# A transformer block's state-space stage: x, z and gates from rounded high and low parts, two buffers for the convolution, weights split in the stage before, and one set of expert weights loaded later

## The reference, cut to what matters

```
normed = layernorm(x, ln1_g, ln1_b)
r = normed @ Wr + br
alpha = sigmoid(r[..., 0:1])
xs, z = split(normed @ Win, 2)
y = causal depthwise convolution of xs with 4 taps, + cb
ssm_out = (silu(y) * sigmoid(z)) @ Wout
gate = sigmoid(normed @ Wgate)          # of the attention branch
blended = ls1 * ((1 - alpha) * ssm_out + alpha * attn_out)
```

## Time and profile before

| what | us |
|---|---|
| median of 3 runs (1224.36 to 1227.06) | 1226.8 |
| the profiled execution | 1225.03 |
| its span, first to last instruction | 1223.3 |
| merge phase | 505 to 536 |
| state-space phase | 536 to 598 |
| self-attention phase | 599 to 729 |
| busy over the span: TensorE, VectorE, ScalarE, GpSimd | 1081.9, 783.1, 649.1, 801.1 |

### The profile page before, as it was taken

The page is one execution under the profiler, slowest core; times in us unless marked ns, Lnnn a source line. Parts: engine busy times, 40 slices in busy tenths (PEclk is TensorE's granted clock), DMA queues, the critical chain, the costliest instruction groups (busy, mean ns, idle before and its releaser), DMA issues. The chain is left out here.

```text
span 1223.3 us, 27556 instructions
## 1 busy us (share of the span) xinstructions
PE 1081.9 (88%) x8144; PEld 973.9 (80%) x8145; DVE 783.1 (64%) x2337; ACT 649.1 (53%) x1499; POOL 801.1 (65%) x835
## 2 busy tenths in 40 slices
PE   4799999999999999879889954899999833999998
PEld 2599999999999999768667743688888622899897
DVE  5566666666666666565456558976776556664663
ACT  1565655655556565153367755766666442553451
POOL 0487777777777778224578750677777503789895
PEclk9899999999999999789899986899999965999999
DMA  4212111111221211089000032133333247645520
GB/s 115 78 53 70 56 56 52 53 54 52 62 63 52 68 57 46 28 214 371 7 1 0 0 59 83 34 53 52 52 52 52 39 143 226 191 119 113 156 45 10
DMA packets 72147, 94.27 MB, mean 77 GB/s; under 512 B 14828, under 2 KB 52160, under 8 KB 72096
## 3 DMA queue, kind: packets, MB, share of 16 engines
q1 hardware_dynamic: 53584, 73.00, 18.7%
q0 software_dynamic: 16032, 20.62, 10.5%
q10 hardware_dynamic: 2480, 0.03, 0.1%
HBM read 73.69 MB, written 22.18 MB: 78 GB/s over the span
## 5 line engine op out<-in xcount | busy, mean ns | idle before, releaser
L1860 POOL DMA_INDIRECT e_x<-rows,source x71 | 76.1, 1071 | 102.1 <-DMA rows<-weight 40.3
L428 PE MATMUL xa_ob<-xa_v,xa_pT 128*128 128x65 f32 x1024 | 135.1, 276 | 0.2 <-DVE xa_pT L653 0.2
L495 POOL TENSOR_TENSOR xa_qbd<-qs,xw_c_mask8s 128x512 fp32r<-128x512 f32 x128 | 131.8, 1051 | 2.3 <-ACT xa_pr L583 2.2
L566 ACT ACTIVATE xa_kT<-xa_kvp,xw_bk 128x258 fp32r<-128x258 f32 x128 | 61.2, 478 | 131.5 <-PE xa_kvp L382 123.9
L583 ACT ACTIVATE xa_pr<-xa_pr,xa_nm 128x257 f32<-128x257 f32 x256 | 109.6, 500 | 34.4 <-DVE xa_nm L649 34.3
L428 PEld LDWEIGHTS xa_ob<-xa_v,xa_pT 128*128 128x128 f32 x1024 | 126.5, 194 | 0.3 <-DVE xa_pT L653 0.3
L642 DVE TENSOR_SCALAR_CACHE_REDUCE xa_pr<-xa_sc 128x257 f32<-128x257 f32 x256 | 98.1, 421 | 23.4 <-PE xa_sc L408 23.4
L525 POOL TENSOR_TENSOR xa_ol<-xa_om,xa_tl 128x256 f32<-128x256 f32 x64 | 47.1, 736 | 81.7 <-DVE xa_rinv L670 81.5
L1865 POOL DMA_INDIRECT base<-e_y,place x39 | 71.6, 1837 | 36.4 <-DVE e_y L2148 19.5
L2527 PE MATMUL e_hb<-e_xTs,e_w1s 128*128 128x512 f32 x384 | 90.9, 396 | 1.9 <-issue 1.9
L653 DVE TENSOR_SCALAR xa_pT<-xa_ptp 128x512 f32<-128x512 f32 x128 | 87.7, 685 | 7.2 <-PE xa_ptp L417 3.2
(11 more groups left out here) (360 smaller groups left out, 3289.9 us busy)
## 6 DMA issues: line engine op xcount, KB each, us to landing
e_w<-in_F_W SPq DMA_DIRECT2D x16, 1024.0 KB, 8.0
w<-in_W SPq DMA_DIRECT2D x24, 512.0 KB, 8.7
xa_ctx<-in_ctxT SPq DMA_DIRECT2D x32, 257.0 KB, 3.0
xa_ctx<-in_ctxT SPq DMA_DIRECT2D x64, 128.5 KB, 3.1
xa_vb<-vlx SPq DMA_DIRECT2D x64, 128.0 KB
rows<-xs_oT SPq DMA_DIRECT2D x8, 512.0 KB, 4.4
xs_oT<-in_x SPq DMA_DIRECT2D x4, 512.0 KB, 5.8
base<-xs_oT SPq DMA_DIRECT2D x4, 512.0 KB, 3.4
```

Source lines behind the costliest of these rows:

```text
L428: mm = pe.matmul(ob[:, 65 * g:65 * g + 65], pT[:, par, g, t, :], v[:, vs, t, g, :], start=(g == 0 and t == 0), stop=(g == G - 1 and t == 1 ...
L495: pool.tensor_tensor(dst, src, msk, ALU.mult).then_inc(q_ready, 1)
L1860: return pool.indirect_dma_start(out=out, out_offset=None, in_=rows, in_offset=bass.IndirectOffsetOnAxis(ap=index, axis=0))
```

## The change

In the state-space phase x, z and the gates are made from parts. A number is split into a high part, rounded to the type fp32r by writing it in that type, and a low part, the rest. A product is then three matmuls in fp32r: high by high, high by low, low by high. The weights are split by GpSimd at the beginning of the merge phase (`split_state_space_weights`: two copies and two subtractions), and SyncE issues the loads of the weights ahead of all else in that phase. The rows of step 0 are split by GpSimd in the merge phase too (`split_first_rows`), behind `nT_stored` 2 and ahead of its four DMAs. The rows of every later step are split in the step before: ScalarE writes the high part, at the head of its step, and GpSimd subtracts. The copy to `nS` goes away.

`xp`, `y` and `sz` get two buffers. So the copy of x waits for the convolution two steps back, and the convolution for yz and sy of two steps back. GpSimd waits with yz for the convolution and Sigmoid of z, and for sy only ahead of gT. The last two steps are written out, and the loop has two turns.

The parts, y and sz lie in the place of `w2`, the first experts' W2, which is therefore loaded by SyncE at the start of the self-attention phase.

```diff
@@ merge_phase
         @block.sync
         def _(sp):
+            load_early(sp)
             for i in range(NG):
                 sp.wait_ge(x1_ready, 2 * i + 2)
                 sp.dma_start(base[...], xs[...]).then_inc(base_written[i], 16)
-                if i == 0:
-                    load_early(sp)
         @block.gpsimd
         def _(pool):
+            split_early(pool)
+            pool.wait_ge(nT_stored, 2)
+            split_rows(pool)
             for i in range(NG):
...
+def split_state_space_weights(pool, w, parts):
+    pool.wait_ge(w.loaded, w.total)
+    for a, b in ((w["Wzx"], parts["zx"]), (w["Wgr"], parts["gr"])):
+        pool.tensor_copy(b[:, 0], a[:]).then_inc(parts["high"], 1)
+    for n, (a, b) in enumerate(((w["Wzx"], parts["zx"]), (w["Wgr"], parts["gr"]))):
+        pool.wait_ge(parts["high"], n + 1)
+        pool.tensor_tensor(b[:, 1], a[:], b[:, 0], ALU.subtract).then_inc(parts["low"], 1)
+
+def split_first_rows(pool, nT, parts):
+    pool.tensor_copy(parts["nS"][:, 0, 0], nT[:, :, 0:V2]).then_inc(parts["nh_ready"], 1)
+    pool.wait_ge(parts["nh_ready"], 1)
+    pool.tensor_tensor(parts["nS"][:, 0, 1], nT[:, :, 0:V2], parts["nS"][:, 0, 0], ALU.subtract).then_inc(parts["nl_ready"], 1)
...
@@ state_space_phase
-        xp = p.sb("ss_xp", [P, 2, BS, L + 3])
+        xp = p.sb("ss_xp", [P, 2, 2, BS, L + 3])
+        TERMS = [(k, a, b) for k in range(2) for a, b in ((0, 0), (0, 1), (1, 0))]
...
         @block.tensor
-                        for k in range(2):
-                            mm = pe.matmul(bank[:, h, :], wzx[:, k, o + P * h:o + P * h + P], src[k],
-                                           start=(k == 0), stop=(k == 1))
+                        for n, (k, a, b) in enumerate(TERMS):
+                            mm = pe.matmul(bank[:, h, :], wzx[:, a, k, o + P * h:o + P * h + P], nS[:, par, b, k, :],
+                                           start=(n == 0), stop=(n == 5))
...
-                    for k in range(2):
-                        lhs = nS[:, par, k, P * t:P * t + P]
-                        mm = pe.matmul(gb[:, t, 0:D + 2], lhs, wgr[:, k, :], start=(k == 0), stop=(k == 1))
+                    for n, (k, a, b) in enumerate(TERMS):
+                        mm = pe.matmul(gb[:, t, 0:D + 2], nS[:, par, a, k, P * t:P * t + P], wgr[:, b, k, :],
+                                       start=(n == 0), stop=(n == 5))
...
         @block.gpsimd
+            def low_part(s, par):
+                pool.wait_ge(parts["nh_ready"], s + 1)
+                pool.tensor_tensor(nS[:, par, 1], nT[:, :, bass.ds(s * V2, V2)], nS[:, par, 0], ALU.subtract
+                                   ).then_inc(parts["nl_ready"], 1)
             def step(s, par):
-                pool.tensor_copy(nS[:, par], nT[:, :, bass.ds(s * V2, V2)]).then_inc(nS_ready, 1)
-                pool.wait_ge(sy_ready, s + 1)
+                if not static(s) or s < NS - 1:
+                    low_part(s + 1, 1 - par)
+                pool.wait_ge(conv, s * 8 + 8)
                 pool.wait_ge(z_stored, s + 1)
                 pool.wait_ge(gT_ready, s)
-                pool.tensor_tensor(yz[:], y[:], sz[:], ALU.mult).then_inc(yz_ready, 1)
+                pool.tensor_tensor(yz[:], y[:, par], sz[:, par], ALU.mult).then_inc(yz_ready, 1)
                 pool.wait_ge(yz_ready, s + 1)
+                pool.wait_ge(sy_ready, s + 1)
...
         @block.scalar
+            def high_part(s, par):
+                if not static(s) or s >= 2:
+                    act.wait_ge(g_ready, s - 1)
+                act.activation(nS[:, par, 0], nT[:, :, bass.ds(s * V2, V2)], ACT.Copy).then_inc(parts["nh_ready"], 1)
             def step(s, par):
+                if not static(s) or s < NS - 1:
+                    high_part(s + 1, 1 - par)
                 act.wait_ge(x_ready, s + 1)
-                act.wait_ge(conv, s * 8)
+                if not static(s) or s >= 2:
+                    act.wait_ge(conv, s * 8 - 8)
...
         @block.vector
                 dve.wait_ge(x_stored, s + 1)
-                dve.wait_ge(gT_ready, s)
+                if not static(s) or s >= 2:
+                    dve.wait_ge(yz_ready, s - 1)
+                    dve.wait_ge(sy_ready, s - 1)
...
@@ self_attention_phase
+        @block.sync
+        def _(sp):
+            load_late(sp)
...
@@ build_program
             def load_experts(sp):          # W1 and W3 of the eight experts
...
+            def load_output_weights(sp):   # passed to self_attention_phase as load_late
+                for e in range(E):
                     sp.dma_start(w2[:, 4 * e:4 * e + 4, :],
                                  io["W2"][e].rearrange("(k p) d -> p k d", p=P)).then_inc(w_loaded, 16)
```

More of the change, by code:

```diff
@@ L771, in merge_weights, with merge_phase @@
     return w
-def merge_phase(nc, w, rc, oT, finite, mean, xs, xin, nT, idle, base, base_written, base_added, load_early):
+def merge_phase(nc, w, rc, oT, finite, mean, xs, xin, nT, idle, base, base_written, base_added, load_early, split_early, split_rows):
     with ExitStack() as st:
@@ L993, in state_space_weights, with state_space_parts, there, state_space_phase @@
     return w
-def state_space_phase(nc, w, nT, xb_, sg, r_all, base_added, load_early):
+def state_space_parts(m, place):
+    zx, gr, n = 2 * 2 * 2 * D, 2 * 2 * (D + 2), 2 * 2 * 2 * V2
+    def there(name, shape, at, dt):
+        return m.nc.alloc_sbuf_tensor_at(name, shape, dt, offset=place + 4 * at)
+    return {"zx": there("sw_zx_parts", [P, 2, 2, 2 * D], 0, F32R), "gr": there("sw_gr_parts", [P, 2, 2, D + 2], zx, F32R),
+            "nS": there("sw_n_parts", [P, 2, 2, 2, V2], zx + gr, F32R), "y": there("ss_y", [P, 2, 2, V2], zx + gr + n, F32),
+            "sz": there("ss_sz", [P, 2, 2, V2], zx + gr + n + 4 * V2, F32), "high": m.sem("sw_high"), "low": m.sem("sw_low"),
+            "nh_ready": m.sem("sw_nh_ready"), "nl_ready": m.sem("sw_nl_ready")}
+def split_state_space_weights(pool, w, parts):
[9 more added lines that the diff above has]
+    pool.tensor_tensor(parts["nS"][:, 0, 1], nT[:, :, 0:V2], parts["nS"][:, 0, 0], ALU.subtract).then_inc(parts["nl_ready"], 1)
+def state_space_phase(nc, w, parts, nT, xb_, sg, r_all, base_added, load_early):
     with ExitStack() as st:
         p = Mem(nc, st)
-        wzx, wgr, wos, cw, cb, br = [w[n] for n in ("Wzx", "Wgr", "Wos", "cw", "cb", "br")]
-        nS = p.sb("ss_nS", [P, 2, 2, V2])
-        sz = p.sb("ss_sz", [P, 2, V2])
-        xp = p.sb("ss_xp", [P, 2, BS, L + 3])
-        y = p.sb("ss_y", [P, 2, V2])
+        wos, cw, cb, br = [w[n] for n in ("Wos", "cw", "cb", "br")]
+        wzx, wgr, nS, y, sz = [parts[n] for n in ("zx", "gr", "nS", "y", "sz")]
+        xp = p.sb("ss_xp", [P, 2, 2, BS, L + 3])
         sy = p.sb("ss_sy", [P, 2, V2])
@@ L1015, in state_space_phase @@
         pad_ready = p.sem("ss_pad_ready")
-        nS_ready = p.sem("ss_nS_ready")
         z_ready = p.sem("ss_z_ready")
@@ L1035, in steps, with static @@
                 step(s, s)
-            with eng.Fori(1, NS // 2) as i:
+            with eng.Fori(1, NS // 2 - 1) as i:
                 for j in range(2):
                     step(i * 2 + j, j)
+            for s in range(NS - 2, NS):
+                step(s, s % 2)
+        def static(s):
+            return isinstance(s, int)
         @block.sync
@@ L1046, in _ @@
             pe.wait_ge(w.loaded, w.total)
+            pe.wait_ge(parts["low"], 2)
             def output(s, par):
@@ L1058, in step @@
             def step(s, par):
-                src = [nT[:, k, bass.ds(s * V2, V2)] for k in range(2)]
+                pe.wait_ge(parts["nh_ready"], s + 1)
+                pe.wait_ge(parts["nl_ready"], s + 1)
                 for bank, o, ready, stored in ((xb, 0, x_ready, x_stored), (zb, D, z_ready, z_stored)):
@@ L1139, in step @@
                 dve.wait_ge(x_stored, s + 1)
-                dve.wait_ge(gT_ready, s)
-                yv = y[:].rearrange("p h (b q) -> p h b q", q=L)
+                if not static(s) or s >= 2:
+                    dve.wait_ge(yz_ready, s - 1)
+                    dve.wait_ge(sy_ready, s - 1)
+                yv = y[:, par].rearrange("p h (b q) -> p h b q", q=L)
                 for n in range(4):
                     for h in range(2):
-                        src, tap = xp[:, h, :, 3 - n:3 - n + L], cw[:, h, 3 - n:4 - n]
+                        src, tap = xp[:, par, h, :, 3 - n:3 - n + L], cw[:, h, 3 - n:4 - n]
                         if n == 0:
@@ L1176, in self_attention_weights, with self_attention_phase @@
     return w
-def self_attention_phase(nc, w, rc, nT, sg, r_all, alpha, xb, stats, idle, ws, base, base_added, retired):
+def self_attention_phase(nc, w, rc, nT, sg, r_all, alpha, xb, stats, idle, ws, base, base_added, load_late, retired):
     with ExitStack() as st:
@@ L2757, in build_program @@
             w13 = m0.sb("w13", [P, E * 4, F1])
+            at_w2 = next_place(nc)
             w2 = m0.sb("w2", [P, E * 4, D])
```

27 lines of the change are left out of this document (14 added, 13 removed).

## The result

| | before | after |
|---|---|---|
| median, 13 executions each on one chip, us | 1224.72 (1222.23 to 1227.8) | 1230.51 (1225.06 to 1234.8) |
| ratio of the executions | | 1.0036, 95% interval 1.002 to 1.0053 |
| the profiled execution, us | 1225.03 | 1226.91 |
| its span, us | 1223.3 | 1225.1 |
| first product of the merge to the first normalisation | 23.4 | 26.2 |

Timed again on another chip the changed kernel gave 1.0028 (1.0006 to 1.0049). So it is slower, by 3.4 to 4.4 us. The phases explain 1.6 to 1.9 of it: the merge grew by 3.8 us, the state space shrank by 2.2. The last four lines of the table are differences between rows of the two timelines.

The account below looks back on a forecast made before the run. TensorE was taken to bound the state-space loop, busy 20.70 of 20.70 us. State space -3.2, guard +2.7 and first rows +1.7 gave +1.2 us: 1226.2 us profiled, 1228.0 as median, range 1221 to 1231.5.

Parts of the forecast that it names:

- rival 3: Merge: GpSimd's first-rows work starts only after the whole row of normalisations, +4.2 instead of +1.7 us, total 1230.5; chance 0.18.
- TensorE no longer the bound: State-space loop: rounded matmuls cut TensorE's work to 5.8 us per step, below the 6.70 us period.
- rival 2: Loop and merge: the holds on VectorE hardly matter, -6.5 + 0.5 us, 1220.8 us; chance 0.17.
- The low part holds the convolution: State-space loop: VectorE's first convolution instruction waits for GpSimd's subtraction, period 6.70 us, not 6.15, against 6.93 before.
- x(0): State-space start: the first step's x products, at the low clock, take 2.9 us instead of 3.70, -0.8 us.
- From the copy of x(0) to the last C: State-space loop, first copy of x to the end of the last convolution: 50.1 us instead of 51.87, -1.7 us.
- term (c): End of the state space: yz doesn't wait for the Sigmoid, so gT ends sooner, -0.7 us.
- The guard held: Merge: VectorE's last two predicated copies are held by GpSimd's split of the weights, +2.7 us.
- Rival 1: Merge: the last predicated copies aren't held, the rest as forecast, -1.5 us, 1225.3 us; chance 0.25.
- The first rows: Merge: GpSimd's split of step 0's rows holds VectorE's normalisations and delays the phase's end, +1.7 us.
- Costed at nothing: W2's move, earlier weights' loads, two buffers, longer static code and a larger memset: 0 us.
- Rival 4: State-space loop: TensorE's idle time lowers its clock, 10 us per step, some 18 us more, about 1245; chance 0.02.

Follow-up runs that it names:

- the last two versions: Changed kernel with VectorE low part, shared weights' split, fp32 step 0, parts one step earlier: ratio 0.9954; the same with the loop written out: 0.9955.
- the tiny low part: Changed kernel with the low parts of steps 2 to 7 computed for only 2 of 256 rows per half: ratio 1.0000, median 1225.20 us.
- the five with one hold less: Changed kernel with 2-row low parts 1.0000, weights split behind guard 1.0013, low part on VectorE 1.0015, weights' split shared with ScalarE 1.0011, or fp32 step 0 1.0031.
- the three fastest: Changed kernel with VectorE low part, shared weights' split and fp32 step 0: 0.9983; also with parts one step earlier: 0.9954; also with loop written out: 0.9955.
- its two versions: Kernel before with only W2 loaded in the self-attention: ratio 0.9994; kernel before with only the weights' loads ahead of the writes of base: 0.9997.

## Why the prediction was nearly right

The forecast was +1.2 us by phases, as +4.4 for the merge and -3.2 for the state space; the phases gave +1.6, as +3.8 and -2.2. In time it said 1228.0 us and within 0.2% of before; 1230.5 was measured, 0.36% over (0.28% on the other chip). So "same" was wrong and "slower", to which it gave 0.29, came true: inside the wide range of 1221 to 1231.5, outside the forecast's own of 1226.5 to 1230. That rival 3 names 1230.5 to the tenth is chance, since what it describes didn't happen. The mechanism was right at all three places, three sizes were off, and one term was missing, the clock, which is worth about as much as the whole forecast of +1.2.

1. *TensorE no longer the bound.* Right, but mis-sized: 5.8 us per step by the second experts' pace of 0.113 us; the runs show 5.97 us where it never waits (the last two versions). So 6.15 us, rival 2's period, lies only 0.2 us above TensorE's floor.
2. *The low part holds the convolution.* Right: the tiny low part takes the hold away and 0.7 us per period. The period was forecast at 6.70; from C to C the six came out at 6.82 to 7.05, and the last at 5.57 instead of 6.15. Between copies of x five of the seven are 6.74 to 7.19, not six as foretold; the first is 5.88. In the step shown the low part ended at C + 4.21 instead of C + 3.85: gT ended at C + 2.75 instead of 2.60, and the low part started 0.19 us behind it, not at once, because ScalarE's high part ended only then (C + 2.74, forecast C + 2.4). The 2.84 us from its end to the next C are those of the forecast (2.85).
3. *x(0)* came 0.85 us sooner (forecast 0.8). *From the copy of x(0) to the last C* it was 50.74 us (forecast 50.1, before 51.87). *The end*: gT at C + 2.68 (forecast 2.63). Not forecast: the output product behind it fell into a stretch at the lower clock, and 0.5 us of the gain with it. This is no accident of one trace. TensorE is idle ahead of that product for 2.9 to 3.5 us in the ten traces of the changed kernel and its versions, against 2.13 in the four of the kernel before; the product takes 2.44 to 3.57 us, against 1.97; and from gT's end to the last store it is 3.45 to 4.58 us, against 2.98. So 0.5 to 1.6 us of what a faster loop gains were lost at its end, more than term (c) in most of them.
4. *The guard held, +2.7.* Right: 4.30 and 4.39 instead of 1.33 us, 2.8 us at the first normalisation. In two of the other traces the first copy slipped ahead of the subtraction, and the pair took 3.5 us. Rival 1 (not held) is refuted. Of this the Trainium skill ("SBUF — State Buffer", section "Who interferes with whom") says that VectorE with two SBUF inputs contends with a GpSimd instruction that reads SBUF, and that whoever issues first has the pair for the whole instruction; the runs agree, for the predicated copy too, and in both directions.
5. *The first rows, +1.7.* The normalisations lost 1.3 us, the phase's start 1.0 to 1.3. The sum had added the two GpSimd instructions (1.9 us) with too little overlap. Rival 3 (GpSimd comes in only behind the whole row) is refuted by the cast at 531.67: between two back-to-back normalisations the waiting engine got the ports. The same page's rule of the whole instruction stands; it doesn't make a row of them one instruction. But they don't always change hands: the 2.29 us of the earlier trace rows were two instructions of GpSimd. The `tensor_scalar` issued at 599.53 found a multiplication at work (L1304, 598.78 to 600.05) and was not served when it ended, but only after the memset behind it (601.79). So a hold can be longer than one instruction, and what decides it was not isolated.
6. *Costed at nothing.* W2's move and the loads ahead of the writes: right within the 0.1% that their runs can tell, each shown by a run of its own. The two buffers and the longer static code had none.
7. *Rival 4.* The clock stayed at 1.00 in the loop. But its idea held at the edges and was missing from the sum. Over 101 executions of the kernel before, the mean granted clock is 0.9421, and a clock 0.001 lower goes with 0.49 us more (0.29 to 0.63 chip by chip). The changed kernel's 24 have 0.9395 in the mean, which by that slope is 1.3 us. Together with 1.6 us that makes 2.9 (a little less, since the phases hold 0.5 us of the clock already), of 3.7 us between the means of these executions; the rest is within the spread. The second chip alone says the same: 3.0 us between the means, of which 1.9 by phases and 0.9 by the clock. Over all versions, what the executions lose beyond the phases of their trace is 1.1 to 4.8 us for the changed kernel and the five with one hold less, 0.2 to 0.7 for the three fastest, and -1.1 to 0.7 for the kernel before and its two versions. Which idle time of TensorE lowers the clock was not isolated: the five versions with one hold less had 0.9386 to 0.9410, and the three fastest 0.9417, 0.9426 and 0.9422, where the kernel before beside them had 0.9414 to 0.9434. That is a correlation, and the cause stays open.

So by phases the change lost because it moved TensorE's work onto the pair of engines that share ports; what the time shows beyond the phases goes with the clock, and its cause is open. With the same products from step 1 on, step 0 in fp32, and the new element-wise work put where the other engine is idle, it gains: 1219.97 us, by the ratio 0.46% under the kernel before.

## What to carry to other kernels

Work given to an engine that is "free" is priced by what it holds up on its neighbour: list for each added GpSimd instruction what VectorE issues while it lasts, and charge VectorE up to the whole instruction, or two where they stand back to back. When a bound engine is relieved, work out the floor of the next one from rows of the same stage, not from the best pace elsewhere. Parts needed a step later are, in this loop, best made in the wait that each engine has anyway (behind the Sigmoid of z, behind the convolution), not at the head of the next step.

## What was unexpected of the hardware

- A predicated copy between SBUF tiles is held by GpSimd like an addition of two SBUF inputs: 1.33 us for two became 4.30, 4.39, 4.21, 3.49 and 3.50, according to where GpSimd's row began.
- Two rows of back-to-back instructions on the two engines alternated in the merge: each predicated copy waited for one subtraction, the second subtraction for one copy (1.74 us instead of 1.29), and two normalisations for one GpSimd instruction each. So two short instructions beside two long ones lost twice. Elsewhere the ports didn't change hands: a `tensor_scalar` waited out a multiplication and the memset behind it (2.29 us, where the next one of its size took 0.17).
- Whoever comes second waits, on either side: VectorE's subtraction took 0.94 us behind gT and 0.68 free, GpSimd's product 1.54 us behind VectorE's subtraction and 1.29 free.
- An execution's mean clock goes with more of this kernel's time than the change is worth: 0.49 us per 0.001, with means from 0.930 to 0.948 seen. This is a correlation.
- A full busy row doesn't prove a bound: TensorE counted as busy for all of 6.23 us in one version and for all of 5.98 us in another, with the same products. The distance between the starts of the same group tells it.
